# Cross-attention value sums of a half's eight heads in one place, each as 64 rows by 32 columns, instead of in two places of four heads

## What is computed

```python
q = _heads(x @ Wq + bq); k = _heads(x @ Wk + bk); v = _heads(x @ Wv + bv)
att = jnp.einsum('bhqd,bhkd->bhqk', q, k) * scale            # 16 heads of 16 channels
att = jnp.where(causal[None, None], att, -jnp.inf)
y = jnp.einsum('bhqk,bhkd->bhqd', jax.nn.softmax(att, axis=-1), v)
qc = _heads(x @ Wcq + bcq); kc = _heads(ctx @ Wck + bck); vc = _heads(ctx @ Wcv + bcv)
attc = jnp.einsum('bhqd,bhkd->bhqk', qc, kc) * scale
y = y + jnp.einsum('bhqk,bhkd->bhqd', jax.nn.softmax(attc, axis=-1), vc)
x = x + tanh(g_xattn) * (y @ Wp + bp)
```

## Time and profile before

| | |
|---|---|
| median of 3 runs | 1542.45 us (1542.35 to 1543.42) |
| the profiled execution | 1540.59 us, of it a span of 1538.5 us |
| PE busy / PEld / DVE / ACT / POOL | 1426.7 / 948.6 / 1145.7 / 896.0 / 901.9 us |
| mean granted TensorE clock | 0.989 of full speed |
| cross value matmuls (line 1511) | 256 records, median 594 ns |
| self value matmuls (line 1529) | 2048 records, mean 438 ns |

### The profile page before, as it was taken

How to read it: one execution, slowest core, us unless ns; L and a number is a source line. 1 busy time by engine, 2 the same in 40 slices (tenths; PEclk the granted TensorE clock), 3 DMA queues, 4 the chain that set the end, 5 groups by cost and what they waited for, 6 DMA issues and landing times.

```text
span 1538.5 us, 36199 instructions
## 1 busy us (share of the span) xinstructions
PE 1426.7 (93%) x11288; PEld 948.6 (62%) x11288; DVE 1145.7 (74%) x3026; ACT 896.0 (58%) x1907; POOL 901.9 (59%) x1643
## 2 busy tenths in 40 slices
PE   4899999999999999999999999999979989898997
PEld 3556556655566566555655665665546778787675
DVE  6777887878778887878788787878644555565686
ACT  3466676666667676666667666665723555565210
POOL 4245566664756666575756657475654555665782
PEclk8899999999999999999999999999999999999999
DMA  6745454545454554645464454545555565454794
GB/s 169 198 131 138 140 151 141 172 135 165 135 160 146 157 169 120 183 133 151 134 177 144 136 180 126 159 134 172 178 152 160 169 221 170 150 153 143 230 351 165
DMA packets 184123, 250.01 MB, mean 162 GB/s; under 512 B 32024, under 2 KB 134560, under 8 KB 183936
## 3 DMA queue, kind: packets, MB, share of 16 engines
q1 hardware_dynamic: 149680, 185.60, 42.0%
q0 software_dynamic: 13008, 36.65, 6.6%
q10 hardware_dynamic: 21248, 25.46, 5.0%
HBM read 150.06 MB, written 95.97 MB: 160 GB/s over the span
## 4 chain that ended last, share of the span: by engine, by line
PE 63%; DVE 18%; ACT 11%; issue 5%; DMA 2%; POOL 1%; SPq 0%; DVEq 0%; ACTq 0%; POOLq 0%
PE vector_bank L2025 8%; PE pv_self L1529 8%; DVE nmax L1288 7%; PE scalar_bank L1465 7%; PE vector_bank L1502 5%; PE vector_bank L1575 4%; PE vector_bank L1439 3%; PE vector_bank L1499 3%; ACT q L857 3%; PE scalar_bank L1452 2%; PE scalar_bank L1455 2%; PE scalar_bank L1453 2%; ACT parts L866 2%; PE scalar_bank L2012 2%; ACT parts L873 2%
## 5 line engine op out<-in xcount | busy, mean ns | idle before, releaser
L1288 DVE TENSOR_REDUCE nmax<-vector_bank 128x1 f32<-128x384 f32 (+4 forms) x832 | 511.2, 639 | 74.4 <-PE vector_bank L1502 70.0
L929 ACT ACTIVATE pt<-scalar_bank 128x512 f32<-128x512 f32 x640 | 362.7, 605 | 175.6 <-PE scalar_bank L1465 167.1
L746 POOL TENSOR_SCALAR_AFFINE_SELECT pt<-pt 128x256 f32<-128x256 f32 (+1 forms) x640 | 222.7, 362 | 206.4 <-ACT pt L929 184.4
L1465 PE MATMUL scalar_bank<-stack 99*64 99x512 bf16 (+4 forms) x1280 | 284.2, 319 | 2.3 <-ACT pt L929 1.0
L1502 PE MATMUL vector_bank<-stack 96*128 96x128 bf16 (+3 forms) x1024 | 244.0, 301 | 0.0
L1854 POOL DMA_INDIRECT rows<-pt x143 | 139.1, 973 | 117.3 <-DVE pt L1983 63.2
L1499 PE MATMUL vector_bank<-tri,ident_b 128*128 128x128 bf16 (+2 forms) x704 | 175.3, 249 | 21.5 <-DMA stack<-qk_scratch 10.5
L1529 PE MATMUL pv_self<-pt,vst 128*32 128x512 f32 (+3 forms) x2048 | 161.1, 438 | 0.1
L705 POOL DMA_INDIRECT rows<-xn,slot x128 | 132.8, 1037 | 44.2 <-issue 26.3
L1499 PEld LDWEIGHTS vector_bank<-tri,ident_b 128*128 128x128 bf16 x704 | 67.0, 97 | 145.2 <-DVE nmax L1288 59.9
L2025 PE MATMUL vector_bank<-pt 128*128 128x128 f32 x1144 | 151.2, 275 | 0.1
(11 more groups left out here) (320 smaller groups left out, 2858.9 us busy)
## 6 DMA issues: line engine op xcount, KB each, us to landing
qk_scratch<-parts SPq DMA_DIRECT2D x31, 1200.0 KB, 4.5
stack<-qk_scratch SPq DMA_DIRECT2D x120, 192.0 KB, 3.0
pt<-rows SPq DMA_DIRECT2D x143, 132.0 KB
stack<-qk_scratch SPq DMA_DIRECT2D x248, 72.0 KB, 2.5
stack<-qk_scratch SPq DMA_DIRECT2D x124, 128.0 KB, 3.0
stack<-qk_scratch SPq DMA_DIRECT2D x240, 36.0 KB, 2.1
pt<-rows SPq DMA_DIRECT2D x8, 1024.0 KB, 8.7
stack<-rows SPq DMA_DIRECT2D x8, 1024.0 KB, 11.5
```

The source lines that it names most:

```text
L746: pool.affine_select(out=v, in_=v, compare_op=ALU.is_ge, fill=0.0, base=0, pattern=pat, channel_multiplier=-1).then_inc(masked, 1)
L929: act.activation(dst, bank(kind, b, ("st", c, k))[:, :], ACT.Exp, scale=SCALE).then_inc(scalar_drained, 1)
L1288: dve.tensor_reduce(dst, src, axis=AX, op=ALU.max, negate=True).then_inc(vector_drained, 1)
L1465: return pe.matmul(out, stack[c][0:rows, head, key0:key0 + nk], stack[c][0:rows, head, q0:q0 + nq], start=True, stop=True, **kw)
```

## The change

All eight heads of a half have their cross sums made in one place, at step 14 of the half, by eight fp32 matmuls of 64 rows by 32 columns: head 2j goes from rows 0 to 63 into quarter j of `pv_cross`, head 2j+1 from rows 64 to 127 into quarter j of `pv_self`. The values need no block diagonal any more. So "group" of a cross sum now means even (0) or odd (1) heads; ACT copies both after the exponential of step 15; their transposes are at steps 19 and 23 of half 0 and 18 and 21 of half 1. The self sums of group 0 move from steps 16 and 20 to 18 and 22, and they now wait for the odd cross sums to be out of `pv_self`. The number of copies, transposes and normalisations stays.

```diff
-CUR_UNITS = {(1, 6): ("tU", 0, 1, "x"), (1, 11): ("tU", 0, 1, "s"),
+CUR_UNITS = {(1, 11): ("tU", 0, 1, "s"), (0, 19): ("tU", 0, 0, "x"), (0, 23): ("tU", 0, 1, "x"),
+             (1, 18): ("tU", 1, 0, "x"), (1, 21): ("tU", 1, 1, "x"),
...
-    PV = Events(of_current([(w, c, g) for c in range(KC) for g in range(2) for w in ("x", "s")]), LB, credit=8)
+    PV = Events(of_current([(w, c, g) for c in range(KC) for w in ("x", "s") for g in range(2)]), LB, credit=8)
...
-        vcst = sb("vcst", [P, 3, HU // 2, 64])
+        vcst_all = sb("vcst", [P, 3 * HU // 2 * 64])
+        vcst = vcst_all[:, 0:3 * HU // 2 * 32].rearrange("p (s a d) -> p s a d", s=3, d=32)
...
-                act.activation(usum[w, g][:, :], (pv_cross if w == "x" else pv_self)[:, :], ACT.Copy).then_inc(pv_drained, 1)
+                act.activation(usum[w, g][:, :], (pv_cross if (w, g) == ("x", 0) else pv_self)[:, :], ACT.Copy).then_inc(pv_drained, 1)
...
-                        if c == 1 and k == 3:
-                            unnormalised(kind, b, "x", 0, 1)
                         if c == 1 and k == 8:
                             unnormalised(kind, b, "s", 0, 1)
-                        if k == 18:
-                            unnormalised(kind, b, "x", c, 0)
+                        if k == 15:
+                            for i in range(2):
+                                unnormalised(kind, b, "x", c, i)
                     if cur:
                         unnormalised(kind, b, "s", c, 0)
                         if c == 1:
-                            unnormalised(kind, b, "x", 1, 1)
                             unnormalised(kind, b, "s", 1, 1)
...
-                dst = yc[g][:, :, :, :] if w == "x" else y[:, :, h:h + HEAD_GROUP, :]
+                dst = yc[:, :, g::2, :] if w == "x" else y[:, :, h:h + HEAD_GROUP, :]
                 if w == "x":
-                    dve.wait_ge(y_added, YADD.upto(kind, b, (c, g)) - 2)
+                    dve.wait_ge(y_added, YADD.upto(kind, b, (c, 0)) - 1)
...
-            def pv_cross_products(kind, b, c, g):
-                pe.wait_ge(pv_drained, PV.upto(kind, b, ("x", c, g)) - 2)
-                pe.wait_ge(scalar_drained, SU.upto(kind, b, ("st", c, len(GROUP) * g + 1)))
-                for jp in range(2):
-                    last = pe.matmul(pv_cross[64 * jp:64 * jp + 64, :], vcst[:, c and 1 + b % 2, 2 * g + jp, :], ct[g][:, jp, :],
-                                     start=True, stop=True)
-                last.then_inc(pv_filled, 1)
+            def pv_cross_products(kind, b, c):
+
+                pe.wait_ge(pv_drained, PV.upto(kind, b, ("x", c, 0)) - 1)
+                pe.wait_ge(scalar_drained, SU.upto(kind, b, ("st", c, len(GROUP) + 1)))
+                for j in range(HU // 2):
+                    for i, ps in enumerate((pv_cross, pv_self)):
+                        rows = slice(i * TC, (i + 1) * TC)
+                        last = pe.matmul(ps[32 * j:32 * j + 32, :], vcst[rows, c and 1 + b % 2, j, :], ct[j // 2][rows, j % 2, :],
+                                         start=True, stop=True)
+                        if j == HU // 2 - 1:
+                            last.then_inc(pv_filled, 1)
...
-                    pe.wait_ge(pv_drained, PV.upto(kind, b, ("s", c, g)) - 2)
+                    pe.wait_ge(pv_drained, PV.upto(kind, b, ("s", c, g)) - 1)
...
-                    if k > 0:
-                        pv_cross_products(kind, b, c, 0)
-                    elif c == 1:
-                        pv_cross_products(kind, b, 0, 1)
...
-                if k in (16, 20):
-                    for kt in KT_ORDER[(k - 16) // 2:(k - 12) // 2]:
+                if k == len(GROUP) + 2:
+                    pv_cross_products(kind, b, c)
+                if k in (18, 22):
+                    for kt in KT_ORDER[(k - 18) // 2:(k - 14) // 2]:
                         pv_self_products(kind, b, c, 0, kt)
...
-                    transpose_sums(kind, b, c, 0, "x")
                     if c == 1:
-                        pv_cross_products(kind, b, 1, 1)
                         for kt in KT_ORDER:
                             pv_self_products(kind, b, 1, 1, kt)
```

More of the change, by code:

```diff
@@ L183, in vector_units @@
         if prev:
-            out += [("tU", 1, 1, "x"), ("tU", 1, 1, "s")]
+            out += [("tU", 1, 1, "s")]
         if cur:
@@ L189, in vector_units @@
         if cur:
-            out += [("tU", 0, 0, "x"), ("tU", 0, 0, "s")]
+            out += [("tU", 0, 0, "s")]
         if nxt:
@@ L195, in vector_units @@
         if cur:
-            out += [("tU", 1, 0, "x"), ("tU", 1, 0, "s")]
+            out += [("tU", 1, 0, "s")]
         return out
@@ L218, in attention_phase @@
                   LB, credit=4)
+    NORM = Events(lambda kind: ([("s", 1, 1)] if PARTS[kind][0] else []) +
+                  ([("x", 0, 0), ("x", 0, 1), ("s", 0, 0), ("s", 0, 1), ("x", 1, 0), ("x", 1, 1), ("s", 1, 0)]
+                   if PARTS[kind][1] else []), LB)
     SPLIT = Events(of_next([0, 1]), LB)
@@ L285, in attention_phase @@
         usum = {(w, g): usum_all[:, 2 * g + i, :] for i, w in enumerate(("x", "s")) for g in range(2)}
-        recip = {w: sb(f"recip_{w}", [P, QT, HEAD_GROUP]) for w in ("x", "s")}
+        recip = {(w, g): sb(f"recip_{w}{g}", [P, QT, HEAD_GROUP]) for w in ("x", "s") for g in range(2)}
         y = sb("y", [P, QT, H, D])
-        yc = [sb(f"yc{g}", [P, QT, HEAD_GROUP, D]) for g in range(2)]
+        yc = sb("yc", [P, QT, HU, D])
         yT = sb("yT", [P, KC, T])
@@ L621, in _ @@
                         1.0).then_inc(setup_pool, 1)
[L622 removed]
+            pool.memset(vcst[:, :, :, D:D + 1], 1.0).then_inc(setup_pool, 1)
             pool.wait_ge(setup_pool, 11)
[L624 to L626 removed]
             pool.memset(wr[:, :, E:32], 0.0).then_inc(router_padded, 1)
@@ L711, in split_max @@
                 n = MSPLIT.upto(kind, b, (c, g))
-                pool.wait_ge(vector_drained, VD.start(kind, b) - (0 if kind == "first" else 2) if (c, g) == (0, 1) else
+                pool.wait_ge(vector_drained, VD.start(kind, b) - (0 if kind == "first" else 1) if (c, g) == (0, 1) else
                              VD.upto(kind, b, ("sm", c, LAST_SM[g])))
@@ L880, in unnormalised @@
                     act.wait_ge(vector_filled, VU.start(kind, b))
-                elif PARTS[kind][0]:
+                elif w == "s" and PARTS[kind][0]:
                     act.wait_ge(vector_filled, VU.upto(kind, b, ("tU", 1, 1, w)))
+                else:
+                    act.wait_ge(vector_filled, VU.start(kind, b))
                 act.wait_ge(pv_filled, PV.upto(kind, b, (w, c, g)))
-                act.activation(usum[w, g][:, :], (pv_cross if w == "x" else pv_self)[:, :], ACT.Copy).then_inc(pv_drained, 1)
+                act.activation(usum[w, g][:, :], (pv_cross if (w, g) == ("x", 0) else pv_self)[:, :], ACT.Copy).then_inc(pv_drained, 1)
             def turned_rows(kind, b, name):
@@ L1092, in cross_values @@
                 twin = 1 + (LN.upto(kind, b, 0) - 1) % 2
-                for half_, col in ((0, 0), (1, 32)):
+                for half_ in range(2):
                     rows = slice(half_ * TC, (half_ + 1) * TC)
                     last = dve.tensor_tensor(
-                        vcst[rows, 0:twin + 1:twin, :, col:col + D],
+                        vcst[rows, 0:twin + 1:twin, :, 0:D],
                         ps[rows, 0:C].rearrange("p (s a i d) -> p s a i d", s=KC, i=2, d=D)[:, :, :, half_, :],
@@ L1320, in body @@
                 if prev:
-                    for w in ("x", "s"):
-                        normalise(kind, b, 1, 1, w)
+                    normalise(kind, b, 1, 1, "s")
                 if kind == "pro":
@@ L1344, in body @@
                     if cur:
-                        for w in ("x", "s"):
-                            normalise(kind, b, c, 0, w)
+                        normalise(kind, b, c, 0, "s")
             over_batches(dve, body)
@@ L1436, in transpose_sums @@
                 ps = claim_v(kind, b, ("tU", c, g, w))
-                pe.wait_ge(pv_drained, PV.upto(kind, b, (w, c, g)) if (c, g) != (1, 1) else PV.start(kind, b) - (w == "x"))
+                pe.wait_ge(pv_drained, PV.upto(kind, b, (w, c, g)) if (w, c, g) != ("s", 1, 1) else PV.start(kind, b))
                 for t in range(QT):
@@ L1666, in body @@
                 if prev and not nxt:
-                    for w in ("x", "s"):
-                        transpose_sums(kind, b, 1, 1, w)
+                    transpose_sums(kind, b, 1, 1, "s")
                 if kind == "pro":
```

20 lines of the change are left out of this document (8 added, 12 removed).

## The result

The changed kernel takes 1628.7 us (median of 4 runs, 1624.5 to 1629.8), the one before 1542.4 on the same chip: a ratio of 1.055, 95% interval 1.0524 to 1.0576. It is slower, as forecast, but by 86 us instead of 39. Its profiled execution takes 1629.8 us, its span 1628.1.

The account below looks back on a forecast made before the run. It took PE and DVE to set the pace in alternate stretches, the clock playing no part. Half 0's +1.6 and half 1's +1.0 made +2.6 us per batch, times 15 +39 us: 1581 us, range 1552 to 1597.

Parts of the forecast that it names:

- The place's price: Step 14 of each half: all eight cross tiles run together, in two passes plus layout changes, 1.1 us.
- the wait for ACT's copy at the end of half 1: After half 1's last score unit: PE idles about 1.3 us until ACT has copied (s,1,0) out of the bank.
- DVE's gain in half 1 up to step 12: Half 1, step 6: the transpose and normalisation of (x,0,1) leave, so DVE's pace gains 0.62 us.
- the end and its projections: End of half 1: transpose and cross place go, saving only 0.13 us; next projections: one transpose fewer, -0.44 us.
- (6): Half 1, step 18: self sums wait for ACT to empty `pv_self`; between 0 and 0.5, taken as +0.2 us.
- (1): Half 0, step 12: the cross place goes, under DVE's pace; DVE gains only its wait, -0.24 us.
- (2): Half 0, step 14: the new place, 1.1 us, stands under DVE's pace and costs nothing.
- (5): Half 0: the longer PE stretch gives DVE time and some PE idle goes; 0 to 0.6, taken as -0.3 us.
- (3) to (5): Half 0: self sums from step 16 to 18, +1.73; transposes, +0.44; some PE idle time gone, -0.3 us.
- row tiles apart: Rival: tiles on different rows don't run together, the place takes 2.0 us; 1594 us, chance 0.14.
- PE's work is all that counts: Rival: DVE's stretches shrink with PE's work, each batch gains 1.4 us; 1520 us, chance 0.12.
- half of it is hidden: Rival: half 0's moved self sums half covered, 0.5 us given back elsewhere; +1.2 us per batch, 1560 us, chance 0.16.

Follow-up runs that it names:

- r4: Changed kernel with the self sums (s,1,1) made in the free bank of the even cross sums, with ACT's copy and PE's wait to match; 1643.6 us, ratio 1.058.
- r5: Changed kernel with even and odd heads' banks exchanged and ACT's two copies split, behind the exponentials of steps 15 and 18; 1624.2 us, ratio 1.050.
- r1: Kernel before with only the self sums of group 0 moved, from steps 16 and 20 to 18 and 22; 1602.1 us, ratio 1.034.
- r6: Changed kernel with the cross place at step 16, copies behind step 17, self sums at 20 and 22, one half 1 transpose at 19; 1616.0 us, ratio 1.046.
- r7: Changed kernel with the eight matmuls of the cross place made twice over, in both halves; 1654.1 us, ratio 1.070.
- r3: Changed kernel with POOL's router scale and split of the row maxima in half 0 behind the sixth mask instead of the tenth; 1626.4 us, ratio 1.049.
- r8: Changed kernel with the edits of r3, r4 and r5 together; 1596.0 us, ratio 1.034.
- r12: Changed kernel with 5 unread filler matmuls while PE waits at the transpose of the row maxima, step 16 of half 0; 1621.4 us, ratio 1.051.
- r11: Kernel before with four row tiles per place, (x,1,1) place at step 20, (s,1,1) in its bank, (x,1,0) copied behind step 16, POOL's order altered; 1593.6 us, ratio 1.032.
- r9: Changed kernel with 10 unread filler matmuls while PE waits at the transpose of the row maxima, step 16 of half 0; 1635.9 us, ratio 1.057.

## Why the prediction was right in direction and wrong in size

**What held.** The place's price (1.02 us against 1.1); the wait for ACT's copy at the end of half 1 (1.26 us by r4, "about 1.3"); that nothing comes of the places taken away at steps 0 and 12 of half 1 (DVE's waits took the room at step 13); the self sums' move in half 0 (1.81 against 1.73); DVE's gain in half 1 up to step 12 (-0.49 against -0.62); the end and its projections (-0.72 against -0.57). Step 17 of half 0 is 16.6 us after the first exponential (589.87 against 573.24), 16.1 before: no earlier, as promised. The Trainium skill, "TensorE: Matmul & The Clock Gate", Part 3, has matmuls on different tiles of the array run at the same time; the 1.02 us of the eight tiles agree. The Trainium skill, "TensorEngine Tiling (Array Packing)", section "PSUM Bottleneck", says that the copy out of PSUM may become the bottleneck; the end of half 1 agrees, where PE waits for a copy and is 1.26 us shorter with another bank (r4).

**The step that failed: the move of the self sums in half 1, (6).** Of this move the prediction priced one thing only: "The self sums at step 18 wait for ACT to empty `pv_self`", +0.2 with bounds 0 and 0.5. ACT's part came out at 0.46 us (r5, where the copies no longer stand ahead of the exponentials), inside these bounds. The move itself had no term, and it costs 1.24 us alone (r1). I looked for the wait at the instruction that had moved and priced what it waits for. I didn't ask what it had covered where it stood: at step 16 of half 1 its 1.64 us lay over ACT's and DVE's emptying of the transposed rows, and without it PE runs into that. For half 0 I had asked just this, and there the price was right. The two don't simply add up in the changed kernel: from the score unit of step 16 to the row maximum of step 17 it takes 626.40 - 624.78 = 1.62 us, of which 0.85 is work (2.58 less 1.73, r1), so the lost cover is 0.77 there. r6, with the place at step 16 (and the copies and self sums later), gets 1.16 us back. Half 1 and what follows up to the next batch came out at +2.33 us instead of +1.0: 14 x 1.33 = 19 us.

**Half 0, (1), (2) and (5).** These hoped for -0.54 us in all, and the place free. Half 0 came out at +2.64 instead of +1.6. Step 17 tells where: it comes 0.50 us later in the half, not 0.24 earlier, and from there to the first projection it is 598.27 - 589.87 = 8.40 us instead of 6.26, 2.14 more where (3) to (5) have 1.87. So 0.74 us of the excess lie ahead of step 17 and 0.27 behind it. r7 shows a second place half paid, r3 puts 0.24 us on POOL; how the rest divides wasn't tried. The reason behind POOL's part is a chain the prediction didn't follow: from the last mask of half 1 POOL goes through scatters, additions, the low parts and ten masks to the scale at step 16, some 27 us, and that doesn't get shorter when PE's projections do. What PE saves there it loses here (r4), unless POOL's order changes (r8). 14 x 1.0 = 15 us.

**The clock.** "The granted clock is 1.00 in all four, so the clock is no part of it" was true of the kernel before and taken over for the changed one. Nine batches have a stretch at half clock, 12 us net. Windows of batch 2, around step 16 of half 0:

```profile
216.00:219.90 3.90, 1.95 (x17) 1.05 (x19) 3.34 (x9) 2.90 (x7) 3.02 (x10) 1.00 0.59 145
219.90:223.30 3.40, 3.40 (x20) 1.02 (x13) 0.09 (x2) 0.47 (x1) 0.68 (x2) 0.50 0.73 184
223.30:226.00 2.70, 2.70 (x26) 1.77 (x24) 2.32 (x5) 2.10 (x6) 0.37 (x2) 1.00 0.14 36
```

PE is busy for 1.95 of 3.90 us, then does 3.4 us of work at 0.50 (1.2 GHz) and is back at 2.4 GHz. A wait in front of PE's own stretch can thus cost more than its length; r12 shows it for step 16 of half 0. The four stretches of half 1 begin at step 13, ahead of the waits of steps 17 and 18, which therefore don't explain them. The Trainium skill, "TensorE: Matmul & The Clock Gate", Part 1, says that the clock is set by how busy PE has been recently; these rows agree.

**The sum.** The two profiled spans differ by 90 us, the forecast was 39, so 51 are to be explained: 19 + 15 + 12 = 46, and the first and the last batch with 6.7 us, where one more batch of 2.6 was counted, give 4 more. The medians differ by 86 us, 3 less than the spans. The rival "row tiles apart" is out by the trace, "PE's work is all that counts" and "half of it is hidden" by the batch of 72.9 us.

## What to carry to other kernels

When an instruction moves, price the place it leaves as well as the one it comes to: whatever waits it covered there (here a chain through POOL, another through ACT and DVE) become PE's. Follow the other engines' chains across the stage boundary before counting a gain at the end of a stage. And reckon with a new wait of 2 us on PE being dearer than 2 us, where the granted clock falls behind it.

## What the runs showed of the hardware

- At step 16 of half 0, how often the clock is halved goes with the wait ahead of it, not with the work: the wait was 1.82 us in the changed kernel (5 of 14 batches in half 0, four of them behind that step), 2.55 in r4 (11), 1.94 in r11 (10), cut in two by DVE in r3 (none), filled in r9 and r12 (none behind it). It isn't a fixed rule: r5 leaves half 0 as it was and has 2, and each count is of one execution. What lies behind the stretches in half 1, and why r9 and r12 have fewer of them (1 and 1 against 4), stays open.
- Eight tiles of 64 rows by 32 columns, four, or two of 128 by 64 all take about 1 us at 512 columns in fp32: 1.02, 0.99 and 0.96.
